# Two attention cores and a mixture of experts: rows transposed closer behind their attention, and four shared pieces placed in the drain

## The reference, cut to what matters

```python
x = _layernorm(x + _L1_attn_ref(x, Wq, Wk, Wv, Wo))       # "D": 16 heads of 16, causal
x = _layernorm(x + _L1_xattn_ref(x, ctx, ctx))            # "E": the same core, keys and values from ctx
x = _layernorm(x + _L1_ffn_ref(x, ...))                   # "F": 8 experts, top 2, and a shared expert
...
probs = softmax(x @ Wr); routing_weights, selected = top_k(probs, 2)
moe_out = sum over the two chosen experts e of weight * (silu(x Wg[e]) * (x Wu[e])) Wd[e]
shared = sigmoid(x @ Wsg) * (silu(x Sg) * (x Su)) Sd      # inner width 704
out = moe_out + shared
```

## Time and profile before

| | us |
|---|---|
| median of 3 runs (lowest, highest) | 779.85 (777.71, 783.6) |
| the profiled execution, its own time | 774.44 |
| its span, first to last instruction | 772.3 |
| TensorE busy | 672.7 (87%) |
| VectorE busy | 559.9 (73%) |
| ScalarE busy | 489.1 (63%) |
| GpSimd busy | 250.7 (32%) |

### The profile page before, as it was taken

How to read it: one execution, slowest core, us unless ns; L and a number is a source line. 1 busy time by engine, 2 the same in 40 slices (tenths; PEclk the granted TensorE clock), 3 DMA queues, 4 the chain that set the end, 5 groups by cost and what they waited for, 6 DMA issues and landing times.

```text
span 772.3 us, 18597 instructions
## 1 busy us (share of the span) xinstructions
PE 672.7 (87%) x4914; PEld 603.0 (78%) x4915; DVE 559.9 (73%) x2515; ACT 489.1 (63%) x1354; POOL 250.7 (32%) x422
## 2 busy tenths in 40 slices
PE   5899799777774988999999999997799989999982
PEld 5788577634443988999999899996799978888881
DVE  4788588767887547888888999996857565555386
ACT  4456566458771328899999999994355545555443
POOL 4443200223335400122212122223164405555454
PEclk9999899958875999999999999998899999999996
DMA  9950000000003685667766766641044523333162
GB/s 287 359 153 0 1 1 1 1 0 2 0 1 109 186 287 188 194 201 209 215 198 192 194 202 172 163 132 45 15 130 128 165 62 100 97 103 101 48 228 81
DMA packets 66489, 95.61 MB, mean 124 GB/s; under 512 B 11390, under 2 KB 52992, under 8 KB 66304
## 3 DMA queue, kind: packets, MB, share of 16 engines
q1 hardware_dynamic: 63024, 86.51, 37.9%
q0 software_dynamic: 3408, 8.43, 3.1%
HBM read 62.45 MB, written 33.36 MB: 124 GB/s over the span
## 4 chain that ended last, share of the span: by engine, by line
PE 43%; issue 17%; DVE 17%; SPq 9%; ACT 6%; DMA 4%; POOL 2%; DVEq 0%; ACTq 0%; POOLq 0%
PE bank L1905 8%; PE bank L2047 5%; PE bank L1981 5%; SPq L494 5%; PE bank L1891 5%; PE bank L1637 4%; PE bank L2071 3%; PE bank L1998 3%; SPq L490 3%; PE bank L1880 2%; PE bank L2035 2%; PE bank L1921 1%; DVE X L1119 1%; PE bank L2056 1%; POOL rstd L613 1%
## 5 line engine op out<-in xcount | busy, mean ns | idle before, releaser
L937 ACT ACTIVATE late_mem<-bank,smax 128x128 f32<-128x128 f32 x512 | 150.0, 404 | 14.7 <-DVE smax L1373 13.0
L1373 DVE CUSTOM_DVE_ANT_0 bank<-bank,causal 128x128 f32<-128x128 f32 x512 | 132.8, 323 | 18.1 <-issue 16.9
L1905 PE MATMUL bank<-f_mem,late_mem 128*128 128x68 f32 (+3 forms) x1024 | 127.6, 267 | 0.0
L1905 PEld LDWEIGHTS bank<-f_mem,late_mem 128*128 128x128 f32 x1024 | 124.3, 192 | 0.4 <-issue 0.4
L613 POOL TENSOR_TENSOR rstd<-var,power 128x2 f32<-128x2 f32 (+1 forms) x64 | 40.3, 629 | 194.6 <-DVE var L1112 183.7
L947 ACT ACTIVATE late_mem<-bank 128x512 f32<-128x512 f32 x128 | 81.7, 638 | 4.0 <-PE bank L1891 3.1
L1891 PE MATMUL bank<-ident,late_mem 128*128 128x128 f32 x512 | 78.7, 277 | 3.3 <-ACT late_mem L937 3.0
L1373 DVE DVE_READ_ACCUMULATOR2_ANT smax<- 128x1 f32 x512 | 72.5, 142 | 0.0
L1880 PE MATMUL bank<-kz,qs 128*128 128x256 f32 x256 | 63.6, 331 | 3.9 <-DMA kz<-k_E 2.9
L1891 PEld LDWEIGHTS bank<-ident,late_mem 128*128 128x128 f32 x512 | 59.4, 142 | 5.9 <-ACT late_mem L937 5.7
L1981 PE MATMUL bank<-x_hi,w_hi 128*128 128x256 f32 x176 | 51.3, 291 | 1.0 <-DVE x_lo L1431 1.0
(11 more groups left out here) (283 smaller groups left out, 2003.6 us busy)
## 6 DMA issues: line engine op xcount, KB each, us to landing
qs<-q_D SPq DMA_DIRECT2D x64, 128.0 KB, 2.7
kz<-k_D SPq DMA_DIRECT2D x128, 64.0 KB, 2.6
qs<-q_E SPq DMA_DIRECT2D x64, 128.0 KB, 2.8
kz<-k_E SPq DMA_DIRECT2D x128, 64.0 KB, 2.5
xg<-f_mem SPq DMA_DIRECT2D x1, 5031.0 KB, 22.4
late_mem<-xg SPq DMA_DIRECT2D x39, 129.0 KB
q_D<-stage_d SPq DMA_DIRECT2D x8, 512.0 KB, 2.9
k_D<-stage_d SPq DMA_DIRECT2D x8, 512.0 KB, 4.0
```

The lines of the kernel that those rows point to most:

```text
L937: ins = sc.activation(sp[:, g, i, :], bank[g][:, i * P:(i + 1) * P], ACT.Exp, bias=smax[:, g, i:i + 1], scale=-1.0)
L1373: ins = ve.tensor_tensor_reduce(v[:, i, :], v[:, i, :], causal[:, :], -1.0, 3e38, ALU.add, ALU.min, smax[:, g, i:i + 1])
L1905: ins = mm(bank[6][:, h * (DH + 1):to * (DH + 1)], spt[:, g, i, :], vf[:, slot, h:to, :].rearrange("p h d -> p (h d)"), start=True, stop=True)
```

## The change

- `LAG_XP` goes from 5 to 4 and E gets a lag of its own, `LAG_XE` = 3. Statistics and apply of a row are now in one turn (lag 3 in D, 2 in E), copy_row too. The D transpose moves behind xpose_out; on ScalarE `e_high` moves from behind exps(0) to behind exps(1) and evac_ot. VectorE's `e_low` keeps its place between softmax(1) and softmax(2).
- The row copy and the transposed row get tiles of their own (`xe`, `xt1` in late_mem), so that the pieces' buffers are free. The scores of rows 14 and 15 go to bank 3.
- Stages with lag `None` run only in the drain, one call a turn: the first x_high and x_low, and the pieces 0 to 3. The drain has 4 turns on each engine. Weight slices come one turn earlier.
- The routing is cut up: first choice after piece 3, second choice beside piece 4, the exponentials on ScalarE after piece 5, TensorE's count after products(6), blocks and experts' places beside piece 6, rows' places beside 7, weights beside 8, the table beside 9 (before: the choices and the count ahead of gate(0), the rest beside pieces 0 to 3).
- The scatters run on three semaphores instead of two, so each waits for the third before it.

```diff
+COUNT_AT = 6
+NSC = 3
...
+    top = max(lag for lag, _, _ in stages if lag is not None)
 
     def turn(s):
         for lag, one, two in stages:
+            if lag is None:
+                if s >= 2 * n:
+                    one(s - 2 * n)
+                continue
...
-LAG_XP = 5
+LAG_XP = 4
+LAG_XE = 3
...
+        xe = part(late_mem, 4096, [P, 2, D])
+        xt1 = part(late_mem, 4096 + 2 * D, [P, 2, KC, P])
...
+        def score_bank(t):
+            return bank[NG - 1] if isinstance(t, int) and t > B - LAG_XE else bank[7]
...
-                t = s - B
+                t = s - B + 1
...
-                                     (3, inverse_root("D", 1), inverse_root("E", 1)),
-                                     (4, copy_row("D"), copy_row("E"))])
+            pipelined_pair(pool, B, [(LAG_XE + 1, None, keep_xt), (0, values("D", V), values("E", CTX)),
+                                     (3, inverse_root("D", 1), None), (2, None, inverse_root("E", 1)),
+                                     (3, copy_row("D"), None), (2, None, copy_row("E"))])
...
+                    n = (k * B + b) % NSC
+                    wait_past(pool, f"scattered{n}", 16 * ((k * B + b) // NSC))
                     gp.indirect_dma_start(xg, bass.IndirectOffsetOnAxis(ap=idx[:, k, b:b + 1], axis=0),
-                                          X[:, b * DX:(b + 1) * DX], None).then_inc(sem(f"scattered{b % 2}"), 16)
+                                          X[:, b * DX:(b + 1) * DX], None).then_inc(sem(f"scattered{n}"), 16)
...
-                    stages += [(LAG_XP, e_high, None), (2, None, w_high)]
-                if g == 1:
-                    stages += [(2, evac_ot, None), (LAG_XP, None, f_xt)]
-            pipelined_pair(act, B, stages)
...
+                act.wait_ge(sem("F_xt_kept"), UT // P * (t + 1))
...
+            stages = [(None, first_high, None)]
+            for g in range(NG):
+                stages += [both(g, LAG_PT, evac_pt), both(g, 0, exps)]
+                if g == 0:
+                    stages.append((1, None, w_high))
+                if g == 1:
+                    stages += [(2, evac_ot, None), (LAG_XP, e_high, None), (LAG_XE, None, f_xt)]
+            stages.append((None, piece, None))
+            pipelined_pair(act, B, stages)
...
+            act.wait_ge(sem("F_xt_kept"), B)
+            for c in range(LAG_XP, EARLY * NF):
+                piece(c)
+                if c == COUNT_AT - 1:
+                    act.wait_ge(sem("gap"), 2)
+                    sc.activation(g2[:, :, :], g2[:, :, :], ACT.Exp, scale=-1.0).then_inc(sem("gate_exp"), 1)
+                    sc.activation(sgate[:, :], score[:, :, E], ACT.Exp, scale=-1.0).then_inc(sem("gate_exp"), 1)
...
-            pipelined_pair(dve, B, [(LAG_XP + 1, None, f_scores), both(0, 0, softmax), (3, d_stats, e_stats),
-                                    both(1, 0, softmax), (LAG_XP, e_low, None), both(2, 0, softmax),
-                                    (4, d_apply, e_apply), both(3, 0, softmax), (1, heads_out("D"), heads_out("E")),
-                                    (2, None, w_low)])
...
+            def first_low(k):
+                if k == 0:
+                    x_low(0)
+
+            def piece(c):
+                gate(c)
+                if c > 0:
+                    hid_low(c - 1)
+                if c % NF == 3:
+                    x_low(c // NF + 1)
+
+            def pieces(k):
+                if k < LAG_XP:
+                    piece(k)
+
+            pipelined_pair(dve, B, [(None, first_low, None), (LAG_XE + 1, None, f_scores), both(0, 0, softmax), (3, d_stats, None),
+                                    (2, None, e_stats), both(1, 0, softmax), (LAG_XP, e_low, None), both(2, 0, softmax),
+                                    (3, d_apply, None), (2, None, e_apply), both(3, 0, softmax),
+                                    (1, heads_out("D"), heads_out("E")),
+                                    (1, None, w_low), (None, pieces, None)])
...
+            def first_choice():
+                dve.wait_ge(sem("F_score"), B)
+                own.then(ve.tensor_reduce(m3[:, :], s, axis=AX.X, op=ALU.max))
+                ve.tensor_tensor(g2[:, :, :], bcast(m3), s, ALU.subtract).then_inc(sem("gap"), 1)
+                choose(own, s, s, g3, m1)
+
+            def second_choice():
+                choose(own, s, g5, g4, m2)
+                own.then(ve.tensor_tensor(hotb[:, :, :], g3[:, :, :], g4[:, :, :], ALU.add))
+                ve.engine_nop().then_inc(sem("F_routed"), 1)
...
+            first_choice()
+            beside = {LAG_XP: second_choice, COUNT_AT: count_experts, COUNT_AT + 1: place_rows, COUNT_AT + 2: weigh_rows,
+                      COUNT_AT + 3: table_blocks}
+            for c in range(LAG_XP, EARLY * NF):
+                piece(c)
+                if c in beside:
+                    beside[c]()
+                if c % NF == 3 and c > NF:
+                    add_shared(c // NF - 1)
...
+                            pe.wait_ge(sem("F_score"), min(t, B - LAG_XE + 1) if isinstance(t, int) else t)
...
+                if isinstance(t, int) and t > B - LAG_XE + 1:
+                    pe.wait_ge(sem("F_score"), t)
                 for c in range(KC):
-                    ins = mm(bank[7][:, 0:E + 1], xt1[:, slot, c, :], r1[:, c, :], start=(c == 0), stop=(c == KC - 1))
+                    ins = mm(score_bank(t)[:, 0:E + 1], xt1[:, slot, c, :], r1[:, c, :], start=(c == 0), stop=(c == KC - 1))
...
-                    stages.append((LAG_XP, xpose_row("D"), None))
-                if g == 1:
-                    stages += [(2, xpose_out, None), (LAG_XP, None, xpose_row("E"))]
-            stages += [(2, project, None), (LAG_XP, None, f_router)]
-            pipelined_pair(pe, B, stages)
...
+            def downs(c):
+                if c >= 2:
+                    down(c - 2)
+
+            def shared(c0, t1):
+                for c in range(c0, t1 * NF):
                     products(c)
-                    if c == 1:
+                    if c == COUNT_AT:
                         count()
-                    if c >= t0 * NF + 2:
-                        down(c - 2)
+                    if not EARLY * NF <= c < EARLY * NF + 2:
+                        downs(c)
...
+                    stages += [(2, xpose_out, None), (LAG_XP, xpose_row("D"), None), (LAG_XE, None, xpose_row("E"))]
+            stages += [(2, project, None), (None, products, None), (LAG_XE, None, f_router), (None, downs, None)]
+            pipelined_pair(pe, B, stages)
+
+
+            shared(LAG_XP, EARLY)
```

More of the change, by code:

```diff
@@ L104, in turn_of @@
         for lag, *steps in stages:
-            if steps[phase] is not None:
+            if lag is not None and steps[phase] is not None:
                 t = s - lag
@@ L544, in _ @@
             sp_.wait_ge(sem("F_rl"), NRC)
-            for n in range(2):
-                sp_.wait_ge(sem(f"scattered{n}"), 16 * B)
+            for n in range(NSC):
+                sp_.wait_ge(sem(f"scattered{n}"), 16 * len(range(n, 2 * B, NSC)))
             pipelined(sp_, NBLK, [(0, load_block)], 2, 2)
@@ L1020, in route_high, with first_high @@
                 sc.activation(hi[:, at:at + n], r_in[:, c % 2, 0:n], ACT.Copy).then_inc(sem("F_rh"), 1)
-            def normalize(t):
-                act.wait_ge(sem("F_norm"), t + 1)
-                for j in range(UB):
-                    ins = sc.activation(xrow(t * UB + j), rows(acc, t * UB + j, 1), ACT.Identity,
-                                        bias=nbias[:, t % 2, j:j + 1], scale=rstd[:, t % 2, j:j + 1])
-                ins.then_inc(sem("F_x"), 1)
-            x_high(0)
-            act.wait_ge(sem("gap"), 2)
-            sc.activation(g2[:, :, :], g2[:, :, :], ACT.Exp, scale=-1.0).then_inc(sem("gate_exp"), 1)
-            sc.activation(sgate[:, :], score[:, :, E], ACT.Exp, scale=-1.0).then_inc(sem("gate_exp"), 1)
-            act.wait_ge(sem("core_pv"), NG * B + before("E", "pv"))
-            for c in chunks(0, EARLY):
+            def first_high(k):
+                if k == 0:
+                    x_high(0)
+            def piece(c):
                 t, f = divmod(c, NF)
@@ L1042, in _, with normalize @@
                     x_high(t + 1)
+            stages = [(None, first_high, None)]
[7 more added lines that the diff above has]
+            pipelined_pair(act, B, stages)
+            def normalize(t):
+                act.wait_ge(sem("F_norm"), t + 1)
+                for j in range(UB):
+                    ins = sc.activation(xrow(t * UB + j), rows(acc, t * UB + j, 1), ACT.Identity,
+                                        bias=nbias[:, t % 2, j:j + 1], scale=rstd[:, t % 2, j:j + 1])
+                ins.then_inc(sem("F_x"), 1)
+            act.wait_ge(sem("F_xt_kept"), B)
[5 more added lines that the diff above has]
+                    sc.activation(sgate[:, :], score[:, :, E], ACT.Exp, scale=-1.0).then_inc(sem("gate_exp"), 1)
             hid_high(EARLY * NF - 1)
@@ L1414, in f_scores @@
```

(4 more changed lines are left out.)

113 lines of the change are left out of this document (43 added, 70 removed).

## The result

The changed kernel takes 805.61 us (801.28 to 812.38, 4 runs) against 780.58 (777.71 to 783.6, 4 runs) beside it: ratio 1.0349, interval 1.0297 to 1.0401. Forecast were 793 and at most 802. A ratio leaves out as slow every execution over 1.5% above the fastest of its kernel: one each of kernels 3 and 14, two of 15, five of 17.

What follows compares the result with a forecast made beforehand. TensorE was taken to bound the first core and shared pieces, with an idle hole between; the e-query wait's +17 and the drain's -4 made +13, 774.44 to 787.4 profiled, 793 for the median, range 779 to 802.

Steps and rivals of the forecast that it cites:

- Part 1: First core: e_high behind exps(1) makes VectorE wait 1.88 us before e_low, +1.0 a turn, +17 us in sum.
- the walk: Step-by-step timing of a turn and the drain from earlier trace rows: turns about 8.5 us, products(12) near 568.
- the ring through scores(3): First core: closed dependency through softmax(1), exps(1), e_high, e_low and scores(3), argued against the wait being free.
- rival A: Faster: e_high's wait costs nothing if under VectorE's 0.88 us idle, drain brings 4 to 9: 771 to 776; chance 0.14.
- Part 2: Closer rows, with statistics, apply and copy in one turn: cost and gain nothing in the steady turns.
- Part 3: Drain: four pieces start early in TensorE's hole, products(12) 4.8 us earlier, less 0.8 for table loads: gain 4.
- The two added loads: Drain: gate Exp between Silus needs two more table loads of 1.28 us, one in idle time; priced +0.8.
- Part 4: Routing beside pieces, three scatters: first at 561 to 562, 1.5 us apart, last issue near 609; priced at nothing.
- Covered: Scatters end near 609, before the route weights near 620 that hold the block loads, so they cost nothing.
- B: Partly absorbed: TensorE and VectorE overlap more, +0.4 a turn, total +1 to +4, within 1%; 0.18 with forecast's near edge.
- C: Third slot brings nothing: scatters 1.96 us apart end at 623, 5 to 6 after the route weights: 799; chance 0.10.
- The halved clock: Drain: TensorE's 0.50 clock staying through the first pieces would give about 799 us.

Runs made afterwards that it cites:

- kernels 3: The kernel before with three scatters in flight and nothing else changed: 798.74 us, ratio 1.0187.
- 14: Changed kernel, e-query stage back behind exps(0), three scatters, a one-column memset without semaphore or wait behind each: 769.55 us, ratio 0.9853.
- 15: Changed kernel, e-query stage back behind exps(0), three scatters in flight, 32 nops on POOL ahead of the first scatter, none between: ratio 0.9972.
- 17: Word-for-word repeat of the kernel with e-query stage back, three scatters, a nop behind each: five executions at 788.1 to 793.3 us, one at 776.2.
- kernel 4: Changed kernel with e_low moved behind softmax(2) on VectorE, e_high left behind exps(1): 805.83 us, ratio 1.0376.
- Experiment 1: Changed kernel with the e-query row's transpose and e_high moved back (e_high behind exps(0)), three scatters kept: 791.11 us, ratio 1.0154.
- Kernel 5: Changed kernel with the e-query stage back behind exps(0) and two scatters in flight: 778.12 us, ratio 1.0003.
- kernels 11: Changed kernel, e-query stage back behind exps(0), three scatters in flight, a memset of 128x2 on POOL behind each: 776.09 us, ratio 0.9949.
- 13: Changed kernel, e-query stage back behind exps(0), three scatters in flight, a nop on POOL behind each: 773.05 us, ratio 0.9931.
- 18: Word-for-word repeat of the changed kernel with e-query stage back, three scatters, nothing between them: 772.95 us, ratio 0.9937.
- experiments 2: Changed kernel with two scatters in flight instead of three: 799.06 us, ratio 1.0277.
- 10: Changed kernel, e-query stage where the change puts it, with a memset of 512 columns on POOL behind each scatter: ratio 1.0177.
- 8: Changed kernel, e-query stage back behind exps(0), three scatters in flight, a memset of 256 columns on POOL behind each: ratio 0.9929.
- 9: Changed kernel, e-query stage back behind exps(0), three scatters in flight, a memset of 384 columns on POOL behind each: ratio 0.9913.

## Why the prediction was wrong

**Part 1, right, and a little small.** Forecast: +1.0 in turns 4 to 17, a wait of 1.88 ahead of e_low, turns 18 and 19 at 10.3 and 8.6, sum +17. Measured: +1.1 in most turns (8.55 to 8.89, +16.2 over the 14), a wait of 1.76, 9.93 and 9.64, sum +19.8. The 14 turns were under-sized by 2.2, turn 18 over-sized by 0.4 and turn 19 under-sized by 1.0. In turn 19 the granted clock was 0.50 from 450.5 to 457.3, which the walk did not have; in kernel 4, with a clock of 1.00 there, that turn took 8.13. TensorE below 90% was not met (92%), the wait before scores(3) was. Experiment 1 shows that nothing else contributes, experiment 4 that one clause of the reasoning was too simple: the ring through scores(3) sets the turn with or without VectorE standing still, so rival A's condition ("the added wait stays under 0.88") is not the one that decides.

**Part 2, right.** Kernel 5 keeps the closer rows; its turns are 7.49.

**Part 3, right in kind, too small, and its gain spent elsewhere.** Forecast: first product 1.3 us after the last values, products(12) 4 earlier. Measured: 554.09, after values that end near 552.9, so 1.2; products(12) stands 34.6 us after the last head output, against 41.9, 7.3 earlier. The mis-sized term is the way to the first choice: it starts 12.7 us after the last head output where the walk had 16.1 (547 on the scale of before). From there to products(12) it is 21.9 us with VectorE busy for 19.5, against 18.7 plus 2 to 3 forecast; that part came as walked. One piece of the 3.4 is the Silu's table load, which the walk put between the first product and its Silu: ScalarE's rows show that it ran ahead in idle time. The two added loads, as the earlier trace rows, took 1.28 each:

```profile
551.67 1.28 ACT L1009 ACT_TABLE_LOAD   x1
...
569.04 1.28 ACT L1062 ACT_TABLE_LOAD   x1
570.78 1.28 ACT L1009 ACT_TABLE_LOAD   x1
```

The price I took from the row holds: the instruction ahead of the load at 570.78 ends at 570.77, and the Silu behind it starts at 572.08. The Trainium skill (ScalarE: Activation LUTs, What ACT_TABLE_LOAD costs) adds about as much again for a drain of the engine, which would have halved the gain; these rows show none. Carried on to the route weights the gain is 6.1 us, in kernel 5.

**Part 4, the step that failed.** It said that the third slot could only quicken the scatters, that these stay covered behind the route weights near 620, and that nothing else moves. Each clause was about POOL and SP, none about what runs beside them. Scatter times themselves came nearly as forecast: first at 28.8 us after the last head output (forecast 29 to 31), mean interval 1.46 (forecast 1.5). But the route weights ended at 652.49 instead of near 637 (620 plus the 17 of part 1), 65 us after products(12) instead of 51. That is the +13.9, a term priced at nothing. Some 12 to 13 of it is the late hand-over: in kernels 11, 13, 14 and 18, with three slots and a prompt TensorE, the stretch (from the piece's first matmul) is 52.3 to 52.8 us, against 65.2 after and 51.3 before. The direct evidence is experiments 2 and 10, which change nothing but the scatters and bring L from 99.6 to 91.2 and 91.4; 2 is the stronger, since it ran beside kernels that were late. With it out, experiment 10's ratio times 779.85 is 793.7, beside a forecast of 793. That agreement is partly luck: by the profiled spans experiment 10 is 21.1 above the kernel before (793.4 against 772.3), where the sum had +13; +21.1 lies between the first and the last head output (one turn of 10.93 in it) and -1.6 in L.

"Covered" was wrong as well, the other way round: with two slots the scatters do end last (kernel 5). The third slot is worth 2 to 4 us to this drain (L 91.2 with two, 87.0 to 89.2 with three in 8, 9, 11, 13, 14 and 18), which I had priced at nothing. By an estimate from the fit in the Trainium skill (DMA: Bandwidth & Descriptors, Anatomy of one DMA), 2.3 us a scatter, two in flight would outrun POOL. In kernel 2 the scatters took 59.8 us for 31 intervals, 1.93 each, against 1.27 that POOL needs, so the measurement speaks against it here.

**Rivals.** A, B fell with Part 1. C came near in size (799) for a wrong reason: its scatters would have ended late; they ended early. The halved clock that it named did appear, each time behind idle time of TensorE: at 587.0 to 590.4, ahead of the first late count, where it cost products(12) 1.15 us, and at 597.2 to 600.7 and 604.1 to 610.9, behind late ones.

## What to carry to other kernels

When a stage is moved between two engines' lists, follow the ring that its result closes, not the idle time of one engine; moving the other half of the pair (experiment 4) gives nothing back. Ask of every transfer that is made denser what the engines beside it do, and not only when it lands. And run a kernel that beats the old one in a second session, before believing why: here a nop "cured" a stall that came back with the same kernel.

The best version that showed no late execution in these runs and keeps its scatters 1.45 us or more apart is the changed kernel with the e-query stage back behind exps(0), three scatters in flight and a memset of 256 or 384 columns behind each: 0.9929 and 0.9913 of the kernel before. Both were measured in one session only, so by the rule above the gain still has to be repeated.

## What was not expected of the hardware

- TensorE's count reached ScalarE 3.6 and 9.6 us after the recorded end of the last matmul, beside scatters issued 1.27 us apart, with counts 4.27 us apart; in kernels 11, 13, 14 and 18 a waiting Silu starts 0.04 us after that end, in the kernel before at most 0.3.
- Two sessions of one kernel differ by 18 us (experiments 1 and 18: medians 791.11 and 772.95), while the kernel before beside them differed by 1 us (777.54 and 776.63).
- More scatters in flight made the profiled stretch longer, not shorter, where the hand-over was late: L 91.2 with two, 99.6 and 106.0 with three (the changed kernel and 4), 111.5 with four.
- A table load can run ahead of the wait for its activation's data (551.67, the Silu itself at 555.81), or stand behind it: in the kernel before it started at 545.49, after 2.14 us of waiting for the first product.
